# First attention of a fused block: values and relative values in one run and one PSUM bank, both turned halves with a bank of their own

## The reference

```python
dist = jnp.clip(idx[None, :] - idx[:, None], -R, R) + R
pe_k = rel_emb_k[dist]
pe_v = rel_emb_v[dist]
...
score = jnp.einsum('bhqd,bhkd->bhqk', q, k) + jnp.einsum('bhqd,qkd->bhqk', q, pe_k)
attn = jax.nn.softmax(score, axis=-1)
ctx = jnp.einsum('bhqk,bhkd->bhqd', attn, v) + jnp.einsum('bhqk,qkd->bhqd', attn, pe_v)
ctx = jnp.transpose(ctx, (0, 2, 1, 3)).reshape(b, s, d)
return ctx @ W_out + b_out
```

## Time and profile before

| | |
|---|---|
| median of 3 runs | 2506.7 us (2501.7 to 2507.82) |
| profiled execution: its own time, its span | 2507.11 us, 2505.4 us |
| busy share of the span | PE 90%, PEld 70%, DVE 76%, ACT 69%, POOL 34% |
| first attention, 256 units | 444.1 to 1549.4 us |
| late units and the end of the middle stage | 1549.4 to 1663.8 us |

### The profile page before, as it was taken

One profiled execution on the slowest core, in us unless ns is written; L12 is line 12 of the kernel. 1 busy time (PEld: TensorE's weight loads), 2 busy tenths in 40 slices (PEclk: granted clock), 3 DMA queues, 4 the chain that ended last, 5 costly groups with the idle time before them and its releaser, 6 DMA issues. The chain is left out here.

```text
span 2505.4 us, 90533 instructions
## 1 busy us (share of the span) xinstructions
PE 2250.0 (90%) x34464; PEld 1764.0 (70%) x34464; DVE 1914.7 (76%) x7571; ACT 1736.3 (69%) x5614; POOL 843.7 (34%) x911
## 2 busy tenths in 40 slices
PE   6999998799988899899899888779999699999998
PEld 5888887577777777777777676558777466666665
DVE  6777772567777778777777777658888588898888
ACT  2333332677777777777777777866666599999998
POOL 3666665020122211211112212221212556566562
PEclk9999999899999999999999999989999799999999
DMA  7857452666667666676667664013231111111110
GB/s 245 236 157 196 110 117 45 161 163 166 171 165 177 169 173 170 164 171 166 162 173 173 172 168 122 17 66 113 94 117 69 47 27 42 30 36 38 27 38 14
DMA packets 360772, 304.77 MB, mean 122 GB/s; under 512 B 25368, under 2 KB 328856, under 8 KB 358952
## 3 DMA queue, kind: packets, MB, share of 16 engines
q1 hardware_dynamic: 349864, 271.93, 42.6%
q0 software_dynamic: 10496, 27.28, 3.7%
HBM read 166.43 MB, written 132.69 MB: 119 GB/s over the span
## 5 line engine op out<-in xcount | busy, mean ns | idle before, releaser
L823 ACT ACTIVATE probs<-neg_scores,low 128x256 f32<-128x256 f32 (+1 forms) x1152 | 574.3, 500 | 244.2 <-DVE low L959 226.2
L959 DVE CUSTOM_DVE_ANT_0 neg_scores<-scores,rel_bias 128x256 f32<-128x256 f32 x1024 | 373.7, 421 | 244.3 <-PE scores L1121 126.7
L1135 PE MATMUL probsT<-consts,probs 128*128 128x128 f32 x2240 | 361.5, 284 | 54.2 <-ACT probsT_s L839 49.3
L1135 PEld LDWEIGHTS probsT<-consts,probs 128*128 128x128 f32 x2240 | 248.7, 142 | 111.8 <-ACT probsT_s L839 72.4
L774 POOL TENSOR_SCALAR q_heads<-q_raw,consts,q_bias 128x256 f32<-128x256 f32 x128 | 69.7, 558 | 746.6 <-ACT q_raw L805 746.5
L1685 DVE CUSTOM_DVE_ANT_0 neg_scores<-scores,alibi 128x128 f32<-128x128 f32 (+1 forms) x896 | 265.9, 352 | 57.4 <-PE scores L1741 53.5
L275 POOL TENSOR_TENSOR hid<-hid,gate_bc 128x512 f32<-128x512 f32 x160 | 205.7, 1291 | 151.9 <-DVE hid L448 141.9
L301 ACT ACTIVATE ga<-gate_up 128x512 f32<-128x512 f32 x160 | 95.6, 598 | 223.7 <-PE gate_up L514 208.5
L967 DVE COPY rel_s<-scores 128x768 f32<-128x768 f32 x256 | 244.0, 953 | 5.2 <-PE scores L1121 3.8
L1647 ACT ACTIVATE probs<-neg_scores,low 128x128 f32<-128x128 f32 (+1 forms) x448 | 199.6, 448 | 47.7 <-DVE low L1685 45.7
L1111 PE MATMUL scores<-k_sides,q_heads 32*128 32x256 f32 (+1 forms) x2304 | 205.5, 424 | 26.9 <-DVE rel_s L967 21.0
(11 more groups left out here) (205 smaller groups left out, 4942.6 us busy)
## 6 DMA issues: line engine op xcount, KB each, us to landing
rel_rows<-rel_s SPq DMA_DIRECT2D x256, 192.0 KB
rel_bias<-rel_rows SPq DMA_DIRECT2D x256, 192.0 KB, 3.4
gate_bc<-gate_rows SPq DMA_DIRECT2D x32, 1024.0 KB, 10.1
rel_rows<-rel_s SPq DMA_DIRECT2D x256, 128.0 KB
rel_bias<-rel_rows SPq DMA_DIRECT2D x256, 128.0 KB, 3.0
packed<-ffn_in SPq DMA_DIRECT2D x8, 1280.0 KB, 15.0
xe<-packed SPq DMA_DIRECT2D x16, 640.0 KB, 3.9
expert_out<-ye POOLq DMA_DIRECT2D x16, 640.0 KB, 3.2
```

The lines of the kernel that those rows point to most:

```text
L823: act.activation(probs[s % 3][:, j, 0:w], neg[s % 2][:, j, 0:w], ACT.Exp, bias=low[s % 3][:, j:j + 1], scale=-1.0, accum_out=sums[s // UB ...
L959: dve.tensor_tensor_reduce(neg[s % 2][:, j, 0:w], S_ps[:, 512 * j:512 * j + w], bias_of(s)[:, j, :] if s < NU0 else alibi[:, 4 * j + s % 4 ...
L1135: ins = pe.transpose(PT_ps[:, j * P:(j + 1) * P], probs[u % 3][:, j, kt * P:(kt + 1) * P], ident)
```

## The change

- `PT_ps` becomes two banks. `turn(s-2)` transposes both halves in one go, at the start of the step; the second no longer waits for ScalarE's copy of the first.
- `value` and `relative_values` stand one behind the other after the scores, and share the bank `O_ps`: 128 columns for the values of one group, 384 for relative values, in which the third quarter takes the place of the second. So the values leave the bank once a group (a copy of 128 columns) instead of once a block (256), and `z` is masked in two halves of 256 columns instead of one of 512. `ctx_s` and `z` have two buffers.
- The jobs stand between the transposes and the scores. VectorE and ScalarE serve a job in its own step. No two jobs share a step, and each has another place in the block. "context" is what is left of `turn_a`/`turn_b`: two transposes of the inverse sums. The 64 small products over `z` are `turn_relative`, at the end of the steps r = 6 and 7 (32 each, as before).
- The norm is one step later in the odd blocks, the slots ("prefix") and their weights (`slot_weights`) five steps later on VectorE. The scatters wait for other units.
- The keys have one copy instead of two with different biases; ScalarE makes one instead of two of them a block.

```diff
+                if r == 0 and 2 <= b < NB0 + 2:
+                    job_list.append((s, "context", b - 2))
+                if r == 1 and b + 1 < NB0:
                     job_list.append((s, "q", b + 1))
-                if r == 1 and 2 <= b < NB0 + 2:
+                if r == 2 and 2 <= b < NB0 + 2:
                     job_list.append((s, "out", b - 2))
-                if r == 2 and b + 1 < NB0:
+                if r == 3 and b + 1 < NB0:
                     job_list.append((s, "k", b + 1))
-                if r == 3 and b + 1 < NB0:
+                if r == 4 and b + 1 < NB0:
                     job_list.append((s, "v", b + 1))
-                if r == 7 and odd and 3 <= b < nb + 3:
-                    job_list.append((s, "xn2T", (b - 3) // 2))
-                if r == 4 and not odd and 4 <= b < nb + 4:
+                if r == 5 and not odd and 4 <= b < nb + 4:
+                    job_list.append((s, "xn2T", (b - 4) // 2))
+                if r == 6 and not odd and 4 <= b < nb + 4:
                     job_list.append((s, "router1", (b - 4) // 2))
-                if r == 7 and not odd and 4 <= b < nb + 4:
-                    job_list.append((s, "prefix", (b - 4) // 2))
-                if r == 5 and 1 <= b <= nb:
-                    job_list.append((s, "turn_a", b - 1))
-                if r == 6 and 1 <= b <= NB0:
-                    job_list.append((s, "turn_b", b - 1))
+                if r == 5 and odd and 5 <= b < nb + 5:
+                    job_list.append((s, "prefix", (b - 5) // 2))
...
+                job_no[name, b] = 1 + len(job_no)
...
-                            act.wait_ge(rel_valued, min(2 * nb, (u - 8) // 4 + 1))
-                        act.copy(probsT[:, u % UB // 4, u % 4, 0, :, :].rearrange("p j q -> p (j q)"), PT_ps[:, :]).then_inc(moved0, 1)
+                            act.wait_ge(rel_valued, 4 * min(2 * nb, u // 4 - 1))
+                        act.copy(probsT[:, u % UB // 4, u % 4, 0, :, :].rearrange("p j q -> p (j q)"), PT_ps[0][:, :]).then_inc(moved0, 1)
...
-                        act.copy(probsT[:, u % UB // 4, u % 4, 1, :, :].rearrange("p j q -> p (j q)"), PT_ps[:, :]).then_inc(moved1, 1)
+                        act.copy(probsT[:, u % UB // 4, u % 4, 1, :, :].rearrange("p j q -> p (j q)"), PT_ps[1][:, :]).then_inc(moved1, 1)
...
-                    for name, b in jobs_at.get(s - 1, ()):
+                    for name, b in jobs_at.get(s, ()):
                         move(name, b)
...
-                    if s >= 9 and s % 4 == 1 and s // 4 - 2 < 2 * nb:
-                        g = s // 4 - 2
-                        dve.wait_ge(rel_valued, g + 1)
-                        if g >= 2:
-                            dve.wait_ge(spare_full, job_no["turn_b", g // 2 - 1])
-                        dve.tensor_tensor(z[:, g % 2, :].rearrange("p (a q) -> p a q", q=4),
-                                          RV_ps[:, :].rearrange("p (a q) -> p a q", q=4),
-                                          cview["mask_rel"].unsqueeze(1).to_broadcast((P, P, 4)), ALU.mult).then_inc(rel_masked, 1)
+                    g = (s - 7) // 4
+                    if s >= 7 and s % 4 == 3 and g < 2 * NB0:
+                        dve.wait_ge(valued, 4 * g + 4)
+                        if g < 2 * nb:
+                            dve.wait_ge(rel_valued, 4 * g + 1)
+                        if g >= 4:
+                            dve.wait_ge(spare_free, job_no["context", g // 2 - 2])
+                        dve.tensor_copy(ctx_s[g // 2 % 2][:, g % 2 * P:(g % 2 + 1) * P], O_ps[:, 0:P]).then_inc(ctx_moved, 1)
+                    for half in range(2):
+                        g = (s - 8 - 2 * half) // 4
+                        if s >= 8 and s % 4 == 2 * half and 0 <= g < 2 * nb:
+                            dve.wait_ge(rel_valued, 4 * g + 2 * half + 2)
+                            if g >= 4:
+                                dve.wait_ge(spare_full, job_no["context", g // 2 - 2])
+                            at = P + half * P
+                            dve.tensor_tensor(z[g // 2 % 2][:, g % 2, half * S:(half + 1) * S].rearrange("p (a q) -> p a q", q=4),
+                                              O_ps[:, at:at + S].rearrange("p (a q) -> p a q", q=4),
+                                              cview["mask_rel"].unsqueeze(1).to_broadcast((P, P // 2, 4)), ALU.mult).then_inc(rel_masked, 1)
...
-                        if r == 2:
-                            dve.wait_ge(valued, UB * b)
-                            dve.tensor_copy(ctx_s[:, :], O_ps[:, 0:S]).then_inc(ctx_moved, 1)
...
-                    for name, b in jobs_at.get(s - 1, ()):
+                    for name, b in jobs_at.get(s, ()):
...
-                        if name == "turn_b":
+                        if name == "context":
                             n = job_no[name, b]
...
+                            dve.wait_ge(ctx_moved, 2 * b + 2)
                             if b < nb:
-                                link(dve.tensor_tensor(ctx_all[:, :], M_ps[:, 0:S], ctx_s[:, :], ALU.add))
-                                dve.tensor_tensor(ctxT[:, :], ctx_all[:, :], M_ps[:, S:2 * S], ALU.mult).then_inc(spare_free, 1)
+                                link(dve.tensor_tensor(ctx_all[:, :], M_ps[:, S:2 * S], ctx_s[b % 2][:, :], ALU.add))
+                                dve.tensor_tensor(ctxT[:, :], ctx_all[:, :], M_ps[:, 0:S], ALU.mult).then_inc(spare_free, 1)
...
-                        if r == 2:
+                        if r == 3:
                             normal_stats(p)
-                        if r == 3:
+                        if r == 4:
                             normal_begin()
-                        if r == 5:
+                        if r == 6:
                             newton()
                             newton()
-                        if r == 6:
+                        if r == 7:
                             newton()
                             normal_end(p)
...
-                    if b >= 5 and b % 2 == 1 and p < nb // 2 and r == 1:
+                    if b >= 5 and b % 2 == 1 and p < nb // 2 and r == 6:
                         slot_weights(p)
...
+                    if name == "context":
+                        pe.wait_ge(inverted, b + 1)
+                        for qt in range(2):
+                            ins = pe.transpose(M_ps[:, qt * P:(qt + 1) * P], rinv_c[:, qt, :, :].rearrange("p h c -> p (h c)"), ident)
...
                                 ins = pe.matmul(o, every, chosen[:, k, :], start=(k == 0), stop=(i == TP and k == TP - 1))
                             if i < TP:
                                 ins = pe.matmul(o, earlier, chosen[:, i, :], start=(i == 0), stop=True)
-                    if name != "turn_a":
-                        ins.then_inc(spare_full, 1)
+                    ins.then_inc(spare_full, 1)
+
...
-                def turn(u, kt):
-                    if kt == 0:
-                        pe.wait_ge(exped, 4 * (u + 1))
-                        if u >= 1 and width(u - 1) == S:
+                def turn(u):
+                    pe.wait_ge(exped, 4 * (u + 1))
+                    for kt in range(width(u) // P):
+                        if kt == 0 and u >= 1:
+                            pe.wait_ge(moved0, u)
+                        if kt == 1 and second_halves(u):
                             pe.wait_ge(moved1, second_halves(u))
-                        elif u >= 1:
-                            pe.wait_ge(moved0, u)
-                    else:
-                        pe.wait_ge(moved0, u + 1)
-                    for j in range(4):
-                        ins = pe.transpose(PT_ps[:, j * P:(j + 1) * P], probs[u % 3][:, j, kt * P:(kt + 1) * P], ident)
-                    ins.then_inc(turned, 1)
+                        for j in range(4):
+                            ins = pe.transpose(PT_ps[kt][:, j * P:(j + 1) * P], probs[u % 3][:, j, kt * P:(kt + 1) * P], ident)
+                        ins.then_inc(turned, 1)
...
+                    b, g, qt, i = u // UB, u // 4, u // 4 % 2, u % 4
+                    pe.wait_ge(moved0, u + 1)
+                    if second_halves(u + 1):
                         pe.wait_ge(moved1, second_halves(u + 1))
...
+                    if i == 0 and g >= 1:
+                        pe.wait_ge(ctx_moved, g)
+                    if i == 1 and 1 <= g <= 2 * nb:
+                        pe.wait_ge(rel_masked, 2 * g - 1)
+                    if i == 3 and 1 <= g <= 2 * nb:
+                        pe.wait_ge(rel_masked, 2 * g)
...
+                            ins = pe.matmul(O_ps[rows, 0:P], v_of[b % 2][:, kt, i, rows], probsT[:, qt, i, kt, j, :],
...
+                def relative_values(g, step):
+                    qt, quarter = g % 2, (1, 0, 2, 3)[step]
+                    at = P + (quarter + 1) // 2 * P
+                    for G in range(2 * quarter, 2 * quarter + 2):
...
+                                to = at + 64 * (G % 2)
```

(25 more changed lines are left out.)

87 lines of the change are left out of this document (30 added, 57 removed).

## The result

The changed kernel takes 2495.88 us (median of 7 runs, 2491.85 to 2499.09), the kernel before 2506.6 us (7 runs, 2500.64 to 2508.67) on the same chip: ratio 0.9962, 95% interval 0.9951 to 0.9974. That is 10.7 us or 0.4% less, inside the forecast's range, at the lower edge of its likeliest case.

A forecast was written before the change was run, and what follows sets the result against it. It took a two-step round trip of relative scores (8.25 us) and VectorE's long steps to bind. First attention 0, late units -5, end 0 gave 2501 to 2502 against the median, so 2501 us; range 2476 to 2522.

The forecast's parts named there:

- likeliest case: Whole kernel, 48%: the two-step limit and VectorE's odd block hold; 2495 to 2508 us, at 2501.
- The floor: First attention: copy, store and read-back of relative scores hold any two steps to at least 8.25 us, 4.13 each.
- Rival B: First attention, 27%: the two-step limit gives way; 2481 us, full effect 2460.
- Waits for ScalarE gone: First attention: TensorE's 58.9 us of waits for ScalarE in 1000 us go, but most are covered; 1.0 us a pair won.
- The list: First attention, 16 steps of an even and an odd block: 67.9 us before, 69.1 after (33.85 even, 35.25 odd).
- unexplained rest: First attention: 1.0 us a pair between listed 67.9 and measured 68.9, which the change was to win, ends 0 and 1.0.
- First attention, counted 0: First attention: 69.1 us a pair after against 68.9 measured before; +3 us at most if all 1.0 comes back, counted 0.
- `neg_scores` behind `rel_bias` more often than 67 times: First attention, sign: VectorE's `neg_scores` would wait for the `rel_bias` transfer more often than the 67 times before.
- `scores` behind `rel_s`: First attention, sign: TensorE would wait for VectorE's copy `rel_s` in r = 1 to 5, in place of ScalarE.
- Rival C: First attention, 22%: VectorE's work piles up in the odd block, r = 3 to 7 taking 22.3 us, not 20.65; +17, 2524 us.
- Late units, -5 us with ends 0 and -10: Late units: two banks give back most of TensorE's 7.1 us wait for the first half's copy; -5 us.
- The end, 0: Stage's end: last scatter would end near 1661.3, landing about 1662.6, against 1663.3 for the last residual; nothing given back.

The follow-up runs named there:

- one-bank kernel: Changed kernel with one bank for both turned halves, so the second transposes wait for ScalarE's copy of the first: 2842.15 us, ratio 1.046 to the kernel before.
- first `LEAD = 5` kernel: Changed kernel with relative scores computed one step earlier (three steps ahead, not two) and the norm's store one step later: 2632.05 us, ratio 0.9679 to the kernel before.

## Why the prediction was right, and which terms were off

**The floor: right, and the heart of it.** It said that the round trip of the relative scores holds two steps to 8.25 us, so that waits of TensorE for ScalarE are covered. Shortening the distance gave 8.22 us a step; lengthening it took every step of even blocks from r = 1 to 5 to the loop's 3.6 us. Rival B, that the floor gives way by itself, is out: the median two-step sum is 8.61 before and 8.63 after. By my estimate from the figures of the Trainium skill ("DMA: Bandwidth & Descriptors", section "Anatomy of one DMA") the floor would have been no limit; the runs decide for the row of the trace.

As a least value, though, 8.25 us was wrong. Of 254 two-step sums 66 before and 49 after lie under it. It was one reading of a chain that scatters: where `neg_scores` is released by the transfer, it starts 5.3 to 7.6 us behind the copy's end, in the median 6.3 before (72 times) and 6.2 after (60), where the earlier trace rows has 5.9. With VectorE's 2.33 us that makes 8.6, which is the median of the two-step sums.

**Waits for ScalarE gone: right,** and so is the price: nearly nothing. 58.9 us of waits went, and the list's unexplained rest fell from 1.6 us a pair (69.5 measured, 67.9 listed; 1.0 by the one pair that I had read) to 0.7 (69.8 and 69.1). I had let the change win 1.0. The other 1.2 us were lost to the new order, as the list had it. That the 0.9 won are waits for ScalarE is argued: they are a difference of two rests of a list, and a floor of 8.6 us in place of 8.25 would fill such rests too.

**The list: right in sum, wrong in two steps that cancel.** The odd block came as forecast: r = 4 to 7 in the mean 4.39, 4.71, 4.77, 4.30 against 4.2, 4.85, 4.7, 4.35. In the even block I gave r = 0 only 4.0 us, because TensorE would have a start of 0.7; it measured 4.68 in the mean, and TensorE is busy for all of 4.80. I see no such start. And r = 6 was to take 5.5, since VectorE's router work would wait for a product behind the values; it measured 4.86. TensorE is busy throughout and VectorE for 4.64 of 4.81, and VectorE's waits for that product are 0.3 us in 1000. The wait that I added does not exist.

**First attention, counted 0: +6.2 measured** (+7.6 without scatters). The count did not follow from its own list: 69.1 against 68.9 is +3 us if the change wins the whole 1.0, and +17 if it wins none of it, so +3 was the lower end and not the upper one. The measured +6.2 lies between the two. The mechanism is the one named, TensorE's and VectorE's longer steps against the won rest. Of the 6.2 us, 14 pairs at 0.3 us make 4.5.

**`neg_scores` behind `rel_bias` more often than 67 times: wrong,** 56. Likely the longer steps r = 0 and 6 of even blocks, which TensorE now fills, give the transfers time; I did not test that. `scores` behind `rel_s` in its place: right, 134 times, 106 of them in r = 1 to 5.

**Rival C, the odd block's pile: no.** Spreading it gave no time in three settings (0.9978 by 0.9973 on two chips, 0.9734 by 0.9713, and 0.9576 by 0.9574). The first and third fit the floor: where it spans two steps, a long step next to a short one costs nothing. The second has no such floor, and the spread gave nothing there either. That only the sum of VectorE's excess counts in it, as expected, was not tested apart; its step r = 7, which the scatters prolong, went from 9.3 to 10.3 us in the mean.

**Late units, -5 us with ends 0 and -10: mis-sized, -11.1.** I took TensorE's wait for a copy as the measure. It was the wrong engine's. ScalarE is the busiest engine there, and its idle time is what the change can win. Its waits in the kernel before, 1551.70 to 1649.73 us:

```profile
ACT probsT_s L839 <- PE probsT L1135: 7.2, 12, 0.8
ACT probs L823 <- DVE low L959: 4.3, 6, 1.6
ACT probsT_s L845 <- PE probsT L1135: 1.2, 4, 0.5
```

The same after, 1557.41 to 1644.36 us:

```profile
ACT probs L819 <- DVE low L955: 4.6, 7, 1.3
ACT probsT_s L835 <- PE probsT L1136: 1.4, 4, 0.5
```

ScalarE idled 14.5 us (98.03 less 83.58) and now 6.3 (86.95 less 80.62). ScalarE waited 16 times, 8.4 us in all, for transposes into the one bank, 12 times for those of a first half; with two banks 1.4 us are left. That is 8.1 of the 11.1 us; 3.0 are less busy time of ScalarE, part of it the cut (one unit's head more or less). The one-bank kernel shows that the gain needs the second bank; that these waits of ScalarE are the way it comes about is my reading of the rows.

**The end, 0: mis-sized, -2.4.** I set the last scatter at 1661.3, under 1 us from the end. I took each time of the slots from the `neg_scores` of before and kept 11.2 us for the eight scatters; they took 11.1 (1641.40 to 1652.54), but the slots came at 1641.40, and 14.2 us before the end at 1655.55, where I had 13.2. The last scatter ends 3.0 us before it and does not bind, so the end could give back what I took for lost.

**Sum.** +6.2, -11.1 and -2.4 make -7.3 where I had 0, -5 and 0. The two large terms were off by 6 us each in opposite directions, so that the sum came nearer than its parts: that the forecast of -5.7 us met -10.7 this closely is in part luck. Of the -10.7, 2.6 us are the step from the profiled executions (-8.1) to the medians.

**The better kernel.** The changed kernel with `LEAD = 5` beats both, at 0.968 and 0.971 of the kernel before where the change alone has 0.997. Neither of its halves does that: before with `LEAD = 5` has 0.991. It was not run on the first chip.

## What to carry to other kernels

Look for a loop that runs through a transfer and spans several steps, and divide its length by the steps it spans: if the quotient is close to the mean step, waits inside the step are covered, however many us they show, and removing them pays only once the distance is longer. Where an engine is the busiest of its stage, measure a change by that engine's idle time, not by the waits of its neighbours for it. Of two edits that each give 1% or less alone, the second was worth 2.5 to 3% here with the first in.

## What the runs showed of the hardware

**One step in 16 takes 9 us and more on the other chips.** In the first attention on the first chip no step of before and one of after is longer than 6.5 us. On the others, 9 to 14 of the 16 pairs have such a step in the kernels with scatters and `LEAD = 4` or 5, and it is one in which GpSimd issues its scatters: in the changed kernel the odd block's r = 7, in the kernel before r = 3. Here with the one ahead of it, as stretches of the changed kernel's second profile:

```profile
1400.62:1406.15 5.53, 3.04 (x55) 2.33 (x54) 4.40 (x22) 3.04 (x10) 3.91 (x6) 1.00 0.65 160
1406.15:1415.93 9.78, 7.16 (x114) 5.17 (x115) 4.14 (x17) 2.83 (x9) 2.37 (x3) 0.65 0.50 131
```

With it the first attention of the changed kernel takes 1200.4 us instead of the 1113.9 of the first chip. For most of the gaps inside such a step the profile shows no releaser. The timeline of TensorE, ScalarE and VectorE in such a step of the first `LEAD = 5` kernel, whose 32 small products elsewhere take 0.63 us in one piece:

```profile
1053.45 0.26 PE L1169 MATMUL values<-probsT_s,rel_v 128*32 128x64 f32 x2 [0.39 <-issue]
1054.21 0.25 PE L1169 MATMUL values<-probsT_s,rel_v 128*32 128x64 f32 x2 [0.50 <-issue]
1054.87 0.51 ACT L819 ACTIVATE probs<-neg_scores,low 128x256 f32<-128x256 f32 x1 [2.54 <-issue]
...
1059.28 0.29 DVE L972 COPY ctx_s<-values 128x128 f32<-128x128 f32 x1 [2.60 <-issue]
```

Without the scatters the long steps are gone (first attention 1110.7 us, no step over 6.5), and on the same chip the kernel before falls from 2721.8 to 2613.5 us. So the scatters, or the waits left out with them, cause the long steps. With `LEAD = 3` on that chip, scatters in, the same r = 7 takes 8.4 us in the mean where all steps take 8.2: a step of that length hides it. Why on some chips and not on another, and whether it is the engines' instructions that come late, the runs don't show. The 255 transfers of the instruction queues in the first attention take 0.88 us in the mean both on the first chip and on the second; when they were asked for is not in the trace. The rest of the 8% lies behind the middle stage: 964.6 us from the last unit's `neg_scores` to the end without scatters, 852.9 on the first chip. That stage has 128 indirect transfers of its own; that they are the reason there was not tried.

**A round trip through DRAM of about 6 us.** From the end of the copy to the start of the work that reads it back it takes 5.2 to 7.1 us in the `LEAD = 3` kernel, in the median 5.9, and in the median 6.2 to 6.3 in the two kernels on the first chip. With steps of 3.6 us and one step more of distance, `neg_scores` no longer waits for it.
